# A graph-network kernel whose GpSimd gathers also wait, group by group, for TensorE to be done with the fourth group back

## The chip, the cores and the metric

The kernel runs on one core of one Trainium2 chip. The metric is the device time of one execution in microseconds (us), lower is better. Of the kernel before there are three timed runs and one profiled execution.

## What is computed

Two layers on 6250 nodes of 256 features, in float32. Only the first one matters here:

```python
h = batch_norm(layernorm(x) @ w1.T + b1, g1, bt1)     # 6250 x 256
diff = h[src] - h[dst]                                # 200000 edges, sorted by dst
m = segment_max(diff, dst)                            # per node, 0 where there is no edge
hg = gelu(batch_norm(concat([h, m]) @ wg.T + bg))
x = x + batch_norm(hg @ w2.T + b2) + layernorm(x)
x = x + ffn(layernorm(x))                             # 8 experts, three layers each, softmax weights
```

The costly part is `segment_max` with its 200000 gathered rows of 256 floats.

## The kernel before

**Stages.** The program computes z = layernorm(x) @ w1.T with signs folded in, keeps z in SBUF as high and low float32r parts (`zhl`) and writes it to DRAM (`runs[0:N]`). Then comes the scan that is described below, then the small repair of runs that cross a partition border, the gather of every node's maximum (`gm`), the layer with `wg` and `w2`, and the expert network.

**The scan.** The sorted edges are cut into 128 windows of 1564 consecutive edges, one for each partition. Step s handles edge s of every window: a 128 x 256 tile of z rows, which is combined with the row of the step before by `max(previous + penalty, row)`. The steps go through a ring of 46 slots (`STEPS`) in SBUF, in 34 rounds. A round has seven groups of slots (`NG`, `GS`): 8, 8, 6, 6, 6, 6, 6. In what follows round i and group g have the flat number n = 7i + g.

**Who brings the rows.** GpSimd issues one indirect DMA for each step (L698, `ring<-runs,src_i`), except for the last four slots of group 6 in rounds 1 to 32. Those four come from TensorE (`picked`, L1162 and L1164): for each of the 49 node tiles it multiplies z by a 0/1 matrix of 128 x 512 that says which node each of the 512 wanted rows is. So rounds 1 to 32 have 42 gathers each, and rounds 0 and 33 have 46. The picks run in rounds 0 to 31 (`PK` = 32), always for the round that follows.

**The 0/1 matrices** (`oh`). A group of the scan has seven of them, four made by VectorE (`one_hot`, L921) and three by ScalarE (`distance` L721 and `one_hots` L727). There are buffers for two groups (`HOTS` = 14). TensorE does 28 matmuls of 512 columns for a group: an L1162 and an L1164, twice for each of seven matrices, so 14 of L1164. After the last it adds one to the semaphore `s_ohf`, which is 2 at the start. The makers of group n wait for `s_ohf` at n + 1, that is until group n - 2 is done.

**The order on each engine.**

- GpSimd has only the gathers. Ahead of a group's first gather it waits until the stores of the round before have freed the slots (`s_st[g]`), and ahead of every fourth one until the scan is within 21 steps (`LEAD`, semaphore `s_ch`).
- ScalarE goes group by group (`hots`). Between the parts of the 0/1 matrices it copies ring slots two by two to PSUM (`raw`, L739). The first copy of a group waits for all gathers of that group (`s_g`), and the finished matrices L727 stand behind it in the queue.
- VectorE goes group by group as well (`body`): scan steps (`chain`, L914) take turns with 0/1 matrices, with some counting of edges between them.
- SyncE stores each group of the ring after its last scan step (L845), 1 MB or 768 KB, and streams expert weights in rounds 0 to 15.

```python
if i:
    pool.wait_ge(s_st[g], 16 * i)
for k in range(GO[g], GO[g] + by_pool(i, g)):
    if i and (k - GO[g]) % 4 == 0:
        pool.wait_ge(s_ch, STEPS * i + k - LEAD)
    pool.indirect_dma_start(ring[:, k, :], None, runs[0:N, :], ...).then_inc(s_g[g], 16)
```

The two blocks of functions around the change stand here with their line numbers:

Of the kernel before, what the change touches and what calls it, by code (L numbers as in the profile page):

```python
# [44 lines left out]
NG = 7  # L45
# [8 lines left out]
PK = PG  # L54
SLOTS = 7
BYACT = 4
LEAD = 21
HOTS = 2 * SLOTS
DESCS = 4096
BD = (1, 3, 4, 6)  # L60
# [49 lines left out]
def build(nc, io):  # L110
    ctx = ExitStack()
    with ctx:
# [4 lines left out]
        def sem(name):  # L117

            return spare.pop() if spare else ctx.enter_context(nc.semaphore(name))
# [21 lines left out]
        def sub(base, *names_sizes):  # L141
            at, out = base, {}
            for name, size in names_sizes:
                out[name] = at
                at += -(-size // 64) * 64
                assert at <= plan.top, (name, at, plan.top)
            return out
# [86 lines left out]
        def layer_apply(act, out, arr, c):  # L234

            for t in range(BYACT):
# [8 lines left out]

        places = sub(free0, ("zT", MAT), ("gT", 2 * MAT), ("ring", 0), ("src", WIN * 4), ("pen", WIN * 4), ("oh", HOTS * NPE * P * 4),
                     ("acc", KC * NPE * P * 4), ("part", PW * 4), ("part_hi", PW * 4), ("free", 0))
# [56 lines left out]
        rowf = plan.at("rowf", [1, 2 * P], F32, places["oh"] + 4 * KC * CUT * 4)  # L304
        assert 2 * P <= PIECEW and 4 * KC * CUT * 4 + 2 * P * 4 <= HOTS * NPE * P * 4
        node_i = plan.at("node_i", [P, NT], I32, p2["node"])
# [299 lines left out]

        oh = plan.at("oh", [P, HOTS, NPE * P], F32R, places["oh"])
        ids = plan.at("ids", [P, 2, NPE * P], F32, p2["ids"])
# [31 lines left out]
        s_ohd, s_oha, s_ohf, s_ab, s_pe, s_acc0, s_idp = sem("s_ohd"), sem("s_oha"), sem("s_ohf"), sem("s_ab"), sem("s_pe"), sem("s_acc0"), sem("s_idp")  # L640
# [26 lines left out]
        def by_pool(i, g):  # L667

            return GS[g] - (NPE if g == NG - 1 and 1 <= i <= PK else 0)
# [17 lines left out]
        with nc.Block() as block:  # L687

            @block.gpsimd
            def _(pool):  # L690
                for i in range(ROUNDS):
                    for g in range(NG):
                        if i:
                            pool.wait_ge(s_st[g], 16 * i)
                        for k in range(GO[g], GO[g] + by_pool(i, g)):
                            if i and (k - GO[g]) % 4 == 0:
                                pool.wait_ge(s_ch, STEPS * i + k - LEAD)
                            pool.indirect_dma_start(ring[:, k, :], None, runs[0:N, :],  # L698
                                                    bass.IndirectOffsetOnAxis(ap=src_i[:, STEPS * i + k:STEPS * i + k + 1], axis=0)
                                                    ).then_inc(s_g[g], 16)  # L700

            @block.scalar
            def _(act):
# [104 lines left out]
                def columns(n, k):  # L808
                    act.wait_ge(s_tt, 4 * NCH + KC * n + k + 1)
                    _, _, w = piece_of(n)  # L810
                    for a in range(2):
                        r = act.activation(zs[n % 3][:, a, k, 0:w], ps[:, turned(n, k) + a, 0:w], ACT.Copy)
                    r.then_inc(s_tev, 1)
# [293 lines left out]
            def _(pe):  # L1107
# [68 lines left out]
                pe.transpose(ps[:, 6, 0:P], srcf[:], ident[:]).then_inc(s_srcT, 1)  # L1176
                pe.sem_inc(s_ohf, HOTS // SLOTS)
                for c in range(NCH):
# [914 lines left out]
```

## Time and profile before

| | |
|---|---|
| median of three runs | 3012.4 us (3011.11 to 3012.64) |
| the profiled execution: its own time | 3013.89 us |
| its span, first to last instruction | 3012.1 us |
| mean granted TensorE clock | 0.969 |
| TensorE matmuls busy | 2796.6 us (93%) |
| VectorE busy | 2292.7 us (76%) |
| ScalarE busy | 1943.0 us (65%) |
| GpSimd busy | 1484.6 us (49%) |
| the gathers' first and last start | 89.4 and 1912.5 us |

The profiled execution took 1.8 us more than its span, and 1.5 us more than the median. The profile names engines PE (TensorE matmul), PEld (TensorE weight load), DVE (VectorE), ACT (ScalarE), POOL (GpSimd) and SP (SyncE). A row of instructions says for how long the engine had been idle ahead of it and who ended that. Matmuls overlap in the pipeline, so TensorE's busy time says little of how near it is to its peak. A gather's duration on GpSimd is the time in which the engine made it, and its landing comes later.

### The profile page before, as it was taken

What the parts mean: (1) busy time and instruction counts of PE and PEld (TensorE: products, weight loads), DVE (VectorE), ACT (ScalarE), POOL (GpSimd) and SP (SyncE); (2) the same over time, 40 slices, a digit from 0 to 9 for tenths busy, and PEclk for the clock granted to TensorE, in tenths of its full rate; (3) what the DMA queues carried; (4) which work ended last, traced back from release to release, by engine and by line L of the source; (5) the groups of instructions that cost most, each with busy time, mean ns of one, the idle gap of its engine ahead of it and who ended that gap; (6) DMA issues with size and microseconds to landing.
All of it is one profiled execution on the core that took longest, in us unless ns stands there. A gap on an engine that the chain in (4) does not pass through costs nothing. (4 is left out here: it accounts for less than half of the span.)

```text
span 3012.1 us, 40449 instructions
## 1 busy us (share of the span) xinstructions
PE 2796.6 (93%) x14193; PEld 2342.5 (78%) x14193; DVE 2292.7 (76%) x4785; ACT 1943.0 (65%) x2661; POOL 1484.6 (49%) x1550
## 2 busy tenths in 40 slices
PE   6699999999999999999999998789899999999998
PEld 6577777777776777777777777678799999999998
DVE  6887888888787888887878774498677677676766
ACT  5577777777777777777777765416465565655554
POOL 3677777777777777777777777631000000000000
PEclk9899999999999999999999999899899999999999
DMA  8577777777776666676666666411324334243231
GB/s 252 176 265 231 252 244 244 247 238 247 247 246 233 227 221 224 231 229 223 226 222 222 227 207 214 161 53 75 105 105 142 121 111 136 106 142 117 105 116 56
DMA packets 165632, 560.92 MB, mean 186 GB/s; under 512 B 31278, under 2 KB 68950, under 8 KB 149428
## 3 DMA queue, kind: packets, MB, share of 16 engines
q1 hardware_dynamic: 88164, 356.25, 32.9%
q0 software_dynamic: 77264, 202.08, 23.2%
q8 instruction: 112, 1.84, 0.2%
q14 instruction: 92, 0.75, 0.1%
HBM read 321.21 MB, written 237.00 MB: 185 GB/s over the span
## 5 line engine op out<-in xcount | busy, mean ns | idle before, releaser
L698 POOL DMA_INDIRECT ring<-runs,src_i x1436 | 1386.9, 966 | 469.1 <-issue 365.6
L1162 PE MATMUL ps<-oh,zhl 128*128 128x512 f32 x3136 | 1288.8, 411 | 115.7 <-ACT oh L727 103.4
L1164 PE MATMUL ps<-oh,zhl 128*128 128x512 f32 x3136 | 1245.4, 397 | 0.0
L914 DVE SCALAR_TENSOR_TENSOR ring<-ring,pen,ps 128x256 f32<-128x256 f32 x1260 | 598.8, 475 | 303.9 <-ACT ps L739 286.9
L1162 PEld LDWEIGHTS ps<-oh,zhl 128*128 128x128 f32 x3136 | 602.5, 192 | 284.8 <-ACT oh L727 130.6
L1164 PEld LDWEIGHTS ps<-oh,zhl 128*128 128x128 f32 x3136 | 602.8, 192 | 118.8
L921 DVE TENSOR_SCALAR oh<-ps,nodef 128x512 fp32r<-128x512 f32 x896 | 667.6, 745 | 0.0
L739 ACT ACTIVATE ps<-ring 128x512 f32<-128x512 f32 x630 | 370.4, 588 | 310.7 <-DMA ring<-runs,src_i 287.2
L721 ACT ACTIVATE oh<-ids,nodeneg 128x512 fp32r<-128x512 f32 x672 | 455.9, 711 | 27.0 <-PE ps L1164 26.9
L1707 ACT ACTIVATE av<-ps,vecs 128x896 f32<-128x896 f32 x224 | 246.4, 1100 | 325.3 <-PE ps L204 325.3
L727 ACT ACTIVATE oh<-oh,ones 128x1024 fp32r<-128x1024 f32 x448 | 414.7, 926 | 1.9
L1846 DVE TENSOR_TENSOR h2l<-av,h2h 128x896 fp32r<-128x896 f32 x112 | 122.2, 1092 | 148.4 <-ACT h2h L1709 148.1
L2024 PE MATMUL ps<-fw,h2h 128*128 128x256 f32 x784 | 224.5, 286 | 3.4 <-DVE h2l L1846 3.3
L2025 PE MATMUL ps<-fw,h2l 128*128 128x256 f32 x784 | 222.2, 283 | 0.0
L2026 PE MATMUL ps<-fw,h2h 128*128 128x256 f32 x784 | 222.0, 283 | 0.0
L1648 POOL DMA_DIRECT2D y<-in_x x5 | 8.4, 1685 | 412.1 <-DMA y<-res_d 412.1
L1854 DVE SCALAR_TENSOR_TENSOR y<-ps,wv,y 128x256 f32<-128x256 f32 x392 | 168.7, 478 | 52.6 <-PE ps L2026 52.5
L914 DVE SCALAR_TENSOR_TENSOR ring<-ring,pen 128x256 f32<-128x256 f32 x304 | 146.3, 481 | 76.0 <-DMA ring<-runs,src_i 70.9
L1841 DVE SCALAR_TENSOR_TENSOR y<-bo,wv,y 128x256 f32<-128x256 f32 x392 | 173.6, 479 | 1.4 <-issue 0.2
L202 PE MATMUL ps<-h1h,fw 128*128 128x512 f32 x448 | 168.0, 375 | 2.7 <-DVE h1l L1846 2.7
L203 PE MATMUL ps<-hnl,fw 128*128 128x512 f32 x448 | 164.7, 368 | 0.0
L204 PE MATMUL ps<-hnh,fw 128*128 128x512 f32 x448 | 164.6, 367 | 0.0
(294 smaller groups left out, 3976.1 us busy)
## 6 DMA issues: line engine op xcount, KB each, us to landing
runs<-ring SPq DMA_DIRECT2D x170, 768.0 KB, 3.9
fw<-wsp SPq DMA_DIRECT2D x56, 1536.0 KB, 6.5
runs<-ring SPq DMA_DIRECT2D x68, 1024.0 KB, 4.6
ring<-runs,src_i POOLq DMA_INDIRECT x1436, 3.7
ids<-srcT_d SPq DMA_DIRECT2D x32, 256.0 KB, 5.5
res_d<-x_all SPq DMA_DIRECT2D x7, 896.0 KB
y<-res_d SPq DMA_DIRECT2D x7, 896.0 KB, 8.1
part<-in_Wx SPq DMA_DIRECT2D x16, 384.0 KB, 7.1
```

Source lines behind the costliest of these rows:

```text
L698: pool.indirect_dma_start(ring[:, k, :], None, runs[0:N, :], bass.IndirectOffsetOnAxis(ap=src_i[:, STEPS * i + k:STEPS * i + k + 1], axis= ...
L721: return act.activation(oh[:, hot(i, g, v), :], ids[:, bass.ds(h, 1), :].rearrange("p a n -> p (a n)"), ACT.Abs, bias=nodeneg[:, bass.ds(S ...
L727: act.activation(oh[:, slots, :], oh[:, slots, :].bitcast(F32), ACT.Relu, bias=ones[:, 0:1], scale=-1.0).then_inc(s_oha, 1)
L739: act.activation(ps[:, RAWB[J % 2], :], ring[:, k:k + 2, :].rearrange("p s n -> p (s n)"), ACT.Copy).then_inc(s_cp, 1)
L914: dve.scalar_tensor_tensor(out=ring[:, k, :], in0=ring[:, before, :], scalar=pen[:, STEPS * i + k:STEPS * i + k + 1], in1=row, op0=ALU.add ...
L921: dve.tensor_scalar(oh[:, hot(i, g, v), :], ps[:, IDB, :], nodef[:, SLOTS * g + v:SLOTS * g + v + 1], None, ALU.is_equal).then_inc(s_ohd, 1)
L1162: pe.matmul(ps[:, two + k, :], z_hi(g)[:, v, cols], oh[:, hot(i, g, v), :], start=g == 0 and v == 0, stop=False, skip_group_check=True)
L1164: r = pe.matmul(ps[:, two + k, :], z_lo(g)[:, v, cols], oh[:, hot(i, g, v), :], start=False, stop=False, skip_group_check=True)
L1707: act.activation(av[:, m, :], block_banks(m), ACT.Relu, bias=dv(bi, 2 * e + m), scale=dv(sc, 2 * e + m)).then_inc(s_ev, 1)
L2024: pe.matmul(o, h2h[:, k, st], fw[:, b, 0, 2, k, :], start=k == 0, stop=False)
L2025: pe.matmul(o, h2l[:, k, st], fw[:, b, 0, 2, k, :], start=False, stop=False)
L2026: r = pe.matmul(o, h2h[:, k, st], fw[:, b, 1, 2, k, :], start=False, stop=k == KC - 1)
```

## The change

Ahead of the first gather of every group of rounds 2 to 31, GpSimd also waits for TensorE's semaphore `s_ohf`. The value is 7i + g + 3 - 3 = n. With the 2 it starts from, that asks for n - 2 groups done: groups 0 to n - 3. Counted with group n itself as the first, that is the fourth group back.

```diff
--- before.py
+++ after.py
@@ -55,6 +55,7 @@
 SLOTS = 7
 BYACT = 4
 LEAD = 21
+BEHIND = 3
 HOTS = 2 * SLOTS
 DESCS = 4096
 BD = (1, 3, 4, 6)
@@ -692,6 +693,8 @@
                     for g in range(NG):
                         if i:
                             pool.wait_ge(s_st[g], 16 * i)
+                        if 2 <= i < PK:
+                            pool.wait_ge(s_ohf, NG * i + g + HOTS // SLOTS + 1 - BEHIND)
                         for k in range(GO[g], GO[g] + by_pool(i, g)):
                             if i and (k - GO[g]) % 4 == 0:
                                 pool.wait_ge(s_ch, STEPS * i + k - LEAD)
```

No instruction changes its place on any engine, apart from line numbers. On GpSimd's queue, from the last group of round 1 to the first gather of group 1 of round 2, these rows stand in the kernel before (a gather, its shape, and the semaphores it waits for; `x3` stands for three alike in a row):

```order
L698 DMA ring<-runs,src_i 128x256 [waits s_ch,s_st6]
L698 DMA ring<-runs,src_i 128x256
L698 DMA ring<-runs,src_i 128x256 [waits s_ch,s_st0]
L698 DMA ring<-runs,src_i 128x256 x3
L698 DMA ring<-runs,src_i 128x256 [waits s_ch]
L698 DMA ring<-runs,src_i 128x256 x3
L698 DMA ring<-runs,src_i 128x256 [waits s_ch,s_st1]
```

and these in the changed kernel:

```order
L701 DMA ring<-runs,src_i 128x256 [waits s_ch,s_st6]
L701 DMA ring<-runs,src_i 128x256
L701 DMA ring<-runs,src_i 128x256 [waits s_ch,s_ohf,s_st0]
L701 DMA ring<-runs,src_i 128x256 x3
L701 DMA ring<-runs,src_i 128x256 [waits s_ch]
L701 DMA ring<-runs,src_i 128x256 x3
L701 DMA ring<-runs,src_i 128x256 [waits s_ch,s_ohf,s_st1]
```

Only the first gather of each group has got the new wait beside its two old ones, 210 times in all (30 rounds of seven groups).

## Rows read from the trace of the kernel before

**Rows 1.** The profile's page: busy time of each engine over the span.

```profile
PE 2796.6 (93%) x14193; PEld 2342.5 (78%) x14193; DVE 2292.7 (76%) x4785; ACT 1943.0 (65%) x2661; POOL 1484.6 (49%) x1550
```

**Rows 2.** Groups by line: busy us, mean ns, idle before, who ended it.

```profile
L698 POOL DMA_INDIRECT ring<-runs,src_i x1436 | 1386.9, 966 | 469.1 <-issue 365.6 <-DVE ring L914 71.6 <-POOLq L368 31.9
L1162 PE MATMUL ps<-oh,zhl 128*128 128x512 f32 x3136 | 1288.8, 411 | 115.7 <-ACT oh L727 103.4 <-DVE zhl L969 7.2 <-DVE oh L921 4.3
...
L739 ACT ACTIVATE ps<-ring 128x512 f32<-128x512 f32 x630 | 370.4, 588 | 310.7 <-DMA ring<-runs,src_i 287.2 <-DVE ring L914 23.1
```

**Rows 3.** Waits of GpSimd from 250 to 1800 us: total, times, longest.

```profile
POOL ring L698 <- issue: 309.8, 1017, 0.3
POOL ring L698 <- DVE ring L914: 62.8, 206, 0.3
```

**Rows 4.** Line L698: durations in ns (least, median, most), first and last start.

```profile
L698 POOL DMA_INDIRECT ring<-runs,src_i x1436: 952/957/1670, 89.4 to 1912.5; - x180
...
DMA to landing us min/median/max: 2.7/3.7/6.9
```

**Rows 5.** Windows, line L1164: matmuls begun before a round's first gather starts.

```profile
0.00:202.33 202.33, 65.38 (x164) 31.97 (x164) 0.95 0.69 223
...
0.00:522.02 522.02, 301.70 (x756) 146.54 (x756) 0.96 0.71 236
0.00:575.45 575.45, 338.28 (x846) 164.45 (x846) 0.96 0.72 237
...
0.00:894.79 894.79, 572.64 (x1438) 277.63 (x1438) 0.97 0.72 240
...
0.00:1320.12 1320.12, 883.27 (x2226) 427.57 (x2226) 0.97 0.71 236
...
0.00:1745.38 1745.38, 1194.62 (x3010) 578.10 (x3010) 0.97 0.71 233
```

**Rows 6.** Windows, line L698: gathers begun by the same moment.

```profile
0.00:575.45 575.45, 369.69 (x382) 0.96 0.72 237
```

**Rows 7.** Timeline at the start of round 23, 1319.0 to 1320.3 us.

```profile
1319.48 0.40 PE L1164 MATMUL ps<-oh,zhl 128*128 128x512 f32 x1
...
1319.94 0.39 PE L1164 MATMUL ps<-oh,zhl 128*128 128x512 f32 x1
...
1320.12 0.96 POOL L698 DMA_INDIRECT ring<-runs,src_i  x1 [0.30 <-issue]
```

**Rows 8.** Timeline at 1984 to 1986 us: a gather of `gm` waits for TensorE.

```profile
1984.07 1.69 PE L1408 MATMUL ps<-ident,gm 128*128 128x128 f32 x14
...
1986.03 0.95 POOL L1322 DMA_INDIRECT gm<-runs,pos_i  x1 [1.07 <-PE ps L1408]
```

**Rows 9.** Timeline at 547 to 549 us, group 1 of round 8.

```profile
547.17 0.60 ACT L739 ACTIVATE ps<-ring 128x512 f32<-128x512 f32 x1 [6.72 <-DMA ring<-runs,src_i]
...
548.89 0.79 PE L1162 MATMUL ps<-oh,zhl 128*128 128x512 f32 x1 [5.49 <-ACT oh L727]
```

**Rows 10.** Windows: PE, PEld, DVE, ACT, POOL busy (count), granted clock, DMA share, GB/s.

```profile
330.00:333.00 3.00, 0.55 (x4) 0.12 (x2) 1.14 (x3) 1.77 (x3) 2.39 (x3) 1.00 0.99 385
333.00:336.00 3.00, 3.00 (x8) 2.33 (x8) 3.00 (x9) 2.64 (x5) 2.09 (x3) 0.51 0.56 173
550.00:555.00 5.00, 5.00 (x13) 3.86 (x12) 4.85 (x12) 4.64 (x8) 3.83 (x4) 0.50 0.36 105
703.00:706.00 3.00, 0.58 (x4) 0.15 (x2) 1.19 (x3) 1.82 (x3) 2.34 (x3) 1.00 0.93 380
706.00:709.00 3.00, 3.00 (x14) 2.46 (x15) 3.00 (x9) 2.64 (x5) 2.13 (x3) 1.00 0.57 174
```

**Rows 11.** Timeline at the end of the scan, 1912 to 1919 us.

```profile
1912.47 0.96 POOL L698 DMA_INDIRECT ring<-runs,src_i  x1 [0.30 <-issue]
1916.67 2.57 DVE L914 SCALAR_TENSOR_TENSOR ring<-ring,pen 128x256 f32<-128x256 f32 x5 [4.29 <-DMA ring<-runs,src_i]
...
1918.33 0.69 PE L1232 MATMUL ps<-rowf,ones 1*128 1x256 f32 x2
```

## The prediction

> **What bounds the kernel now.** I read the page first. TensorE is busy for 93% of the span and GpSimd for only 49% [rows 1], which points to TensorE. But GpSimd's work ends at 1912 us [rows 4], and its share is an average over the scan and over stages in which it does next to nothing. So I went on to the groups by line. The 1436 gathers of L698 are busy for 1386.9 us, 966 ns each, and the idle time ahead of them is nearly all "issue", which is time in which the engine waited for nothing the profile shows [rows 2]. The waits of GpSimd from 250 to 1800 us say it more sharply: 1223 gathers, none with more than 0.3 us of idle time ahead of it [rows 3]. None of the old waits holds GpSimd up, neither the one for the stores nor the one for the scan. It makes gathers back to back: (1912.5 - 89.4) / 1435 = 1.270 us each [rows 4]. A round of 42 takes 53.3 us.
>
> The others follow it. ScalarE's copies of ring slots wait 287 us for the gathers to land, and the matrices behind them in the queue make TensorE wait 103 us [rows 2]. In one of these places the copy waits 6.72 us and TensorE then 5.49 us [rows 9]. **So the pace of the scan is GpSimd's, and TensorE has time to spare in it.** Time that GpSimd loses is not won back, because it never runs slower than it can. The stage's end hangs on the same queue: last gather at 1912.5 us, last scan step done at 1916.67 + 2.57 = 1919.2 us, with TensorE done at 1919.0 us [rows 11].
>
> **The change, part by part.** It adds 210 waits and takes nothing away. What counts is whether TensorE has finished group n - 3 when GpSimd comes to group n.
>
> *The waits as instructions.* A group's first gather already had two waits and still shows the 0.30 us of any other [rows 7]. They are worked off while the gather before is busy for 0.96 us. I cost a third one at nothing. Without that cover the nearest price is a whole further gap of 0.3 us, 63 us for 210, but the two old waits together show none of it; below nothing is ruled out, since nothing is taken away.
>
> *Where the wait binds.* For the first group of round i, groups 0 to 7i - 3 must be done: 14 x (7i - 2) matmuls of L1164. A window that ends where the round's first gather starts counts those begun. For round 9 the gathers begun are 46 + 8 x 42 = 382, so the next one is its first [rows 6]. Needed are 854, begun are 846: eight short [rows 5]. The same windows for rounds 2 to 31 (first and last in [rows 5]) give as shortage 4, 0, 0, 0, 1, 4, 0, 8, 0, 0, 0, 7, 0, 4, 0, 6, 1, 1, 2, 4, 0, 0, 1, 7, 0, 1, 7, 0, 0, 0: together 58, in 15 rounds.
>
> Even with none short the last one is mostly still running. At round 23 all 2226 have begun [rows 5], but the last ends at 1319.94 + 0.39 = 1320.33 us and the gather started at 1320.12 [rows 7]: 0.21 us late. This is no accident. Group 6 has only two gathers, so from the last gather of group 4 to the next round's first one there are just nine steps of 1.27 us, about as long as landing, copy, matrix and the 28 matmuls take. In rounds 3 and 11 it is done in time.
>
> At the six other groups of a round, read in the same way, GpSimd comes after TensorE's end, except behind a large disturbance (group 4 of round 8 for one). What is waited for there is then missing at the next round's start, so I count round starts only.
>
> *What a wait costs beyond that.* A gather of `gm` that waited for TensorE started at 1986.03 us, after an end at 1984.07 + 1.69 = 1985.76 [rows 8]: 0.27 us.
>
> *The sum.* Pairs of matmuls follow each other by 1319.94 - 1319.48 = 0.46 us [rows 7].
> - 58 pairs short x 0.46 = 26.7 us
> - 28 rounds x (0.21 + 0.27) = 13.4 us
> - in 15 rounds half a pair more, since the next had not begun: 15 x 0.23 = 3.5 us
>
> That makes 43.6 us. It adds up, because a held gather delays its own group's landing, then ScalarE, then TensorE: TensorE is no earlier at the next round's start, relative to GpSimd, than it was.
>
> *TensorE's clock.* In each round TensorE runs dry ahead of group 1, because group 6 came from two gathers and group 1 needs eight. In round 4 it is busy for 0.55 of 3 us and then at a granted clock of 0.51, so half of 2.4 GHz; in round 11 it is busy for 0.58 of 3 us and stays at 1.00 [rows 10]. Nine rounds (3, 7, 9, 13, 15, 17, 21, 25, 28) are spared the gap today, as TensorE is behind in them. When GpSimd waits for TensorE, they have it too. What such a fall leaves at the next round's start lies between nothing and what followed the fall of round 14: at round 15, 1442 needed and 1438 begun [rows 5], four pairs or 1.8 us. Most falls leave a pair or none, so I take 0.5 us, an estimate: 9 x 0.5 = 4.5 us. If the gap never costs anything it is 0, at 1.8 us each it is 16.
>
> The Trainium skill has a rule that weighs more against this change ("TensorE: Matmul & The Clock Gate", section "HAM oscillation — how this bites in real kernels"): idle gaps between bursts put the array back to half clock every time, and its example spends a quarter of its time so. Gaps of one length went both ways here, so the trace agrees in part. By the rule the time would be that of the first rival below.
>
> In all 43.6 + 4.5 = 48 us. Against the profiled execution's 3013.9 us that is 3062 us; against the median of 3012.4 us it is **3060 us**. Late next is only TensorE's own group 4, and behind the waiting gather stand only gathers. What waits for these is ScalarE, VectorE and the stores, all shifted alike. After round 31 nothing waits any more, and the end of the stage shifts as a whole.
>
> **The rivals.**
>
> *A loop through the clock, 3082 us.* GpSimd's wait makes TensorE's gap, the gap halves its clock, and the late TensorE makes GpSimd wait longer. Today the lateness is worked off, since TensorE's round is shorter than 53.3 us. For it: five pauses like that of round 8, with the clock at 0.50 behind it [rows 10], all leave large shortages. Against it: after most falls one pair or none is short. Price: six rounds at (6.5 x 0.46 + 0.71 =) 3.7 us, and 24 at 2.0 us, between the 0.5 of none short and the 2.5 of four: 70 us.
>
> *Waits that are mostly met, 3040 us.* TensorE's ends are modelled and could lie earlier, and the release of a waiting gather might cost nothing. Then only whole missing pairs count, 27 us.
>
> *It does not bind, 3012 us.* If the value asked for one group less, TensorE would have 14 x 0.46 = 6.4 us more, over the 8 x 0.46 + 0.7 = 4.4 us of the worst round start, and nothing would change. Against it stands the code: `s_ohf` starts at 2.
>
> *Fewer gathers under way help, 2999 us.* No row here names what made the gathers of round 8 land late [rows 9]; it may be the crowd of gathers and stores on the DMA engines. With gathers held back it would thin out, and if what makes some gathers longer than 957 ns (up to 1670 ns [rows 4]) is the crowd too, GpSimd's own pace rises. At most that gives 1436 x (966 - 957) ns = 13 us, and it decides only if the waits cost less than 13 us; the 27 us of whole pairs alone are twice that. The Trainium skill says that the engines alternate between the queues fed by software and by hardware ("DMA: Bandwidth & Descriptors", section "SWDGE vs HWDGE vs iDMA"), which would make holding one back a help to the other. No row tells whether it does so here.
>
> **How the numbers follow.** My own forecast gets 0.66 (its own range is 3050 to 3070 us), the loop 0.22, waits mostly met 0.07, no binding 0.03, and the help 0.02. The range goes from 3039 us, whole pairs alone, to 3084 us, the loop at its price and a little over. It leaves out the last two cases and the worst of the loop. A measurement of this kernel can tell 0.2%, 6 us, from no change. Slower gets 0.95, within 0.2% 0.03, faster 0.02.
>
> **What would show it.** In the profile of the changed kernel GpSimd's gathers should have a new releaser, L1164 of TensorE, about 30 to 40 times, for 40 to 60 us with the 0.3 us of the gap in it, nearly always at a round's first group, by 0.5 us or by 2 to 4 us. The gathers should last 966 ns as before, the last one should start at about 1960 us, and what comes after it should take as long as now. The clock should fall to half in more of the thirty rounds. The prediction is wrong if GpSimd shows no such waits, if they add up to 40 us or more and the scan still ends before 1940 us, or if waits of 2 us and more stand at most round starts.

## The result and the profile after

The changed kernel takes 3080.06 us (median of 4 runs, 3071.94 to 3083.20) against 3012.45 us for the kernel before (4 runs, the three known before and one beside the change, 3011.11 to 3012.64). The ratio is 1.0216, with an interval of [1.0204, 1.0228], so it is slower by 67.6 us. The forecast was 3060 us with a range of 3039 to 3084 us. The side and the bound came out as predicted. The price was 20 us too low, outside the 3050 to 3070 us that the forecast gave its own mechanism.

The page of the changed kernel, busy time of each engine, answers to [rows 1]:

```profile
span 3080.7 us, 40449 instructions
...
PE 2813.0 (91%) x14193; PEld 2362.7 (77%) x14193; DVE 2291.3 (74%) x4785; ACT 1943.7 (63%) x2661; POOL 1484.5 (48%) x1550
```

No engine has more work than before, apart from 16 us more of TensorE (2813.0 against 2796.6 us), yet the span has grown by 68.6 us. The 16 us go with more time at the lower clock, see below. The time is in what stands between the instructions. The groups by line (busy us, mean ns of one, idle time ahead of them and who ended it) answer to [rows 2]. The line numbers have moved by three:

```profile
L701 POOL DMA_INDIRECT ring<-runs,src_i x1436 | 1386.4, 965 | 538.5 <-issue 451.8 <-DVE ring L917 53.3 <-POOLq L369 33.4
L1165 PE MATMUL ps<-oh,zhl 128*128 128x512 f32 x3136 | 1298.4, 414 | 168.4 <-ACT oh L730 156.4 <-DVE zhl L972 6.5 <-DVE oh L924 5.1
...
L742 ACT ACTIVATE ps<-ring 128x512 f32<-128x512 f32 x630 | 370.1, 588 | 377.0 <-DMA ring<-runs,src_i 346.9
```

The gathers themselves have kept their length, 965 ns against 966. The idle time ahead of them has grown from 469.1 to 538.5 us, by 69.4 us. That is the whole loss. ScalarE's copies wait 60 us longer for gathers to land (346.9 against 287.2 us), and TensorE waits 53 us longer for ScalarE's matrices (156.4 against 103.4 us). These are followers of a slower GpSimd, and cost nothing by themselves.

GpSimd's waits over the whole span (total, times, longest) show where the 69.4 us are. [rows 3] showed no idle time above 0.3 us in the scan:

```profile
POOL ring L701 <- issue: 451.8, 1260, 4.5
POOL ring L701 <- DVE ring L917: 53.3, 175, 0.3
POOL ring L701 <- POOLq L369: 33.4, 1, 33.4
```

The row "issue" now has a longest one of 4.5 us. The prediction expected TensorE to be named as the releaser. The profile does not name it: it puts the new waits under "issue", time in which nothing visible was waited for. They are found only by the length of the gap. Thirty-seven gathers of the changed kernel stand behind a gap of more than 0.4 us. Less the 0.3 us that every gather has, these holds add up to 68.0 us: 59.0 us at group 0 (29 holds), 5.4 us at group 4 (6 holds), 3.6 us at group 1 (2 holds). All of them are at a group's first gather, where the new wait stands.

Line L701 alone (least, median and longest duration in ns, first and last start; then from issue to landing) answers to [rows 4]:

```profile
L701 POOL DMA_INDIRECT ring<-runs,src_i x1436: 951/957/2606, 90.8 to 1981.3; - x180
...
DMA to landing us min/median/max: 2.7/3.2/7.4
```

The last gather starts at 1981.3 us instead of 1912.5, 68.8 us later, and the span has grown by 68.6 us. What follows the scan takes as long as it did. Holds, last gather and span all say 68 to 69 us.

**One hold closely.** The first group of round 13 is n = 91, so TensorE's groups 0 to 88 have to be done. A window that ends while that gather is held shows all of them begun: 14 x (7 x 13 - 2) = 1246 matmuls of L1167.

```profile
0.00:816.30 816.30, 497.96 (x1246) 242.45 (x1246) 0.95 0.70 232
```

The timeline has the last of them and the gather that waits for it (start, duration, then in brackets the idle time ahead):

```profile
816.16 0.39 PE L1167 MATMUL ps<-oh,zhl 128*128 128x512 f32 x1
...
817.29 0.96 POOL L701 DMA_INDIRECT ring<-runs,src_i  x1 [3.43 <-issue]
```

The matmul ends at 816.16 + 0.39 = 816.55 us and the gather starts at 817.29. So a released gather comes 0.74 us after TensorE's end in the records. The prediction had 0.27 us, from [rows 8]. In the 29 holds at group 0 it is 0.74 us, in the eight at groups 1 and 4 it is 0.99 and 1.03 us: 29 x 0.74 + 8.2 = 29.7 us in all. The remaining 38.3 us are lateness of TensorE: 37.6 us at group 0, and less than 1 us at the other two together. At group 4 five of the six held gathers would have started after TensorE's recorded end, and were held all the same.

ScalarE shows that the end in the records is not what is late. At the end of an earlier group its next 0/1 matrix waits for the same semaphore:

```profile
524.98 0.39 PE L1167 MATMUL ps<-oh,zhl 128*128 128x512 f32 x1
...
525.41 0.72 ACT L724 ACTIVATE oh<-ids,nodeneg 128x512 fp32r<-128x512 f32 x1 [0.90 <-PE ps L1167]
```

It starts at 525.41 us, 0.04 us after 524.98 + 0.39 = 525.37, and so it does in all 15 such places.

**Where the release is spent.** The trace also holds what GpSimd's sequencer does, the part of the engine that takes the instructions in ahead of it. The waits for `s_ch`, and now those for `s_ohf` too, do not stand on the gather: they stand in an instruction of the sequencer's own, `EVENT_SEMAPHORE`, ahead of it. The gather itself carries the wait for `s_st[g]`. Durations of these instructions in ns (least, median, longest), in the kernel before and in the changed one:

```profile
L697 POOLq EVENT_SEMAPHORE  x231: 17/17/17, 141.7 to 1890.5; - x116
```

```profile
L700 POOLq EVENT_SEMAPHORE  x231: 17/3867/13445, 142.9 to 1959.0; - x116
```

Their number is the same, and so is that of all instructions (40449): the new wait has gone into an instruction that was there already. In each of the 37 holds it ends 0.04 us after TensorE's matmul, as fast as ScalarE. The gather starts 0.70 us after that at group 0, and 0.94 to 0.99 us after it at groups 1 and 4. So the release is not late in reaching GpSimd. It is spent between the sequencer's wait and the gather. In the kernel before this wait is over 10.6 us or more ahead of its gather, and nothing of it is seen. In the changed one the first gather of round 3, with 0.72 us between them, is not held, and those with 0.70 us are. Why the groups differ is not known.

**Where TensorE is late.** Round 14 shows the place the prediction spoke of under the clock. ScalarE's first copy and TensorE's next matmul, with their idle time, and the two stretches of 3 us around them (busy time of PE, PEld, DVE, ACT and POOL, then TensorE's clock, the DMA share and GB/s):

```profile
896.49 0.60 ACT L742 ACTIVATE ps<-ring 128x512 f32<-128x512 f32 x1 [5.92 <-DMA ring<-runs,src_i]
...
898.21 0.79 PE L1165 MATMUL ps<-oh,zhl 128*128 128x512 f32 x1 [5.04 <-ACT oh L730]
```

```profile
894.00:897.00 3.00, 0.00 (x0) 0.00 (x0) 0.00 (x0) 0.51 (x1) 2.39 (x3) 0.98 0.92 320
897.00:900.00 3.00, 1.79 (x4) 1.49 (x5) 2.88 (x6) 3.00 (x6) 2.35 (x3) 0.50 0.42 132
```

The copy waited 5.92 us for gathers to land while the DMA engines were 92% busy, TensorE had nothing to do for 5.04 us, and then it went on at a granted clock of 0.50, which is 1.2 of 2.4 GHz. TensorE has gaps of over 4 us ahead of group 0 or 1 in 15 rounds, before in five. The mean granted clock fell from 0.969 to 0.959. In rounds 2 to 31 the clock records hold 139.9 us at half clock in 27 stretches, against 81.9 us in 17 in the kernel before.

Still, TensorE's lateness itself has hardly grown. Read from the trace of the kernel before in the same way, as the end of the last matmul needed less the start of the round's first gather, it is 34.3 us in 28 rounds; in the changed kernel it is 37.6 us. With 0.74 us for each release the old trace alone would have given 55.5 us at the round starts, where 59.0 were measured.

### The profile page after: what moved, and what is told of

Same layout as the page of the kernel before. It is cut to its first block and busy times, and to the rows that moved or that the text cites. A ratio compares the mean times of both kernels' runs of the same rounds, so it can differ in the third digit from the quotient of the medians.

```text
span 3080.7 us, 40449 instructions
## 1 busy us (share of the span) xinstructions
PE 2813.0 (91%) x14193; PEld 2362.7 (77%) x14193; DVE 2291.3 (74%) x4785; ACT 1943.7 (63%) x2661; POOL 1484.5 (48%) x1550
## 5 line engine op out<-in xcount | busy, mean ns | idle before, releaser
L701 POOL DMA_INDIRECT ring<-runs,src_i x1436 | 1386.4, 965 | 538.5 <-issue 451.8
L1165 PE MATMUL ps<-oh,zhl 128*128 128x512 f32 x3136 | 1298.4, 414 | 168.4 <-ACT oh L730 156.4
L1167 PE MATMUL ps<-oh,zhl 128*128 128x512 f32 x3136 | 1256.2, 401 | 0.0
L1165 PEld LDWEIGHTS ps<-oh,zhl 128*128 128x128 f32 x3136 | 610.1, 195 | 330.3 <-ACT oh L730 109.3
L1167 PEld LDWEIGHTS ps<-oh,zhl 128*128 128x128 f32 x3136 | 610.5, 195 | 122.3
L742 ACT ACTIVATE ps<-ring 128x512 f32<-128x512 f32 x630 | 370.1, 588 | 377.0 <-DMA ring<-runs,src_i 346.9
```

The lines of the kernel that those rows point to most:

```text
L701: pool.indirect_dma_start(ring[:, k, :], None, runs[0:N, :], bass.IndirectOffsetOnAxis(ap=src_i[:, STEPS * i + k:STEPS * i + k + 1], axis= ...
L742: act.activation(ps[:, RAWB[J % 2], :], ring[:, k:k + 2, :].rearrange("p s n -> p (s n)"), ACT.Copy).then_inc(s_cp, 1)
L1165: pe.matmul(ps[:, two + k, :], z_hi(g)[:, v, cols], oh[:, hot(i, g, v), :], start=g == 0 and v == 0, stop=False, skip_group_check=True)
L1167: r = pe.matmul(ps[:, two + k, :], z_lo(g)[:, v, cols], oh[:, hot(i, g, v), :], start=False, stop=False, skip_group_check=True)
```

## The experiments

The question was what the 68 us consist of: whether holds add up one to one, what the release is worth, what makes TensorE late (clock or late landings), and whether the wait as an instruction costs anything. The theory that I held, "the count": GpSimd sets the pace, each hold costs TensorE's lateness plus a release, and nothing comes back. The rivals held that it feeds itself through the clock, or that something else than the holds costs the time. The diffs are against the changed kernel.

**A condition of the chip first.** In two of the four batches the kernel before itself took 3589 and 3586 us instead of 3008 to 3015. The results give the chip the number 0 in one of these two batches and in both of the others, and 4 in the second of the two. Whether the number 0 is always the same chip is not on record, so it stays open whether this goes with the chip or with a state of it. Those runs can't be set against the others, so they stand apart, at the end of this section.

### The wait in every fourth round only

```diff
-                        if 2 <= i < PK:
+                        if 2 <= i < PK and i % 4 == 2:
```

> The new wait is kept in rounds 2, 6, 10, 14, 18, 22, 26 and 30 alone. In the kernel before TensorE was 2.1, 0.8, 0.2, 0.2, 0.5, 0.3, 0.2 and 0.4 us behind GpSimd at the starts of these rounds (4.7 us together). Theory C, a hold breeds the next: a hold moves the gathers behind it into other transfers, TensorE runs dry for longer, its clock falls, and it is late again one round on. With three rounds between two holds this has died out, so each costs its own lateness and 0.73 us: 8 x 0.73 + 4.7 = 10.5 us, 3019 to 3027 us. Rival D, each hold costs the same 2.1 us that the changed kernel shows on average, whatever came before: 17 us, 3029 us.

Measured: 3023.62 us against 3008.00 for the kernel before (7 runs), ratio 1.0051 [1.0034, 1.0068], so 15.6 us. GpSimd's waits over the whole span:

```profile
POOL ring L701 <- issue: 382.0, 1207, 2.4
POOL ring L701 <- DVE ring L917: 69.5, 228, 0.3
POOL ring L701 <- POOLq L369: 32.0, 1, 32.0
```

There are 13 holds with 14.2 us: eight at group 0 (10.1 us, as theory C had it) and five at group 4 (4.1 us), which neither theory had. The 15.6 us lie inside the range of C, but nearer to the 17 us of D than to the 10.5 us of C, so the time alone does not decide between them. Idle time ahead of the gathers is 382.0 + 69.5 + 32.0 = 483.5 us, 14.4 over [rows 2]. In the three rounds between, where TensorE could catch up, nothing of it came back, though TensorE has the time. That is as the count says. Against the trace of the kernel before the span has grown by only 9.1 us, since the gathers of this batch were shorter (953 against 957 ns in the median, 4.9 us in sum). A round with the wait costs 15.6 / 8 = 2.0 us, and 67.6 / 30 = 2.3 us where all have it. So rounds may disturb their neighbours a little, by 0.3 us.

### A tighter wait

```diff
-BEHIND = 3
+BEHIND = 2
```

> The wait asks for one group more, n - 2. TensorE ends a group 6.5 to 7.5 us after the one before, so at a round start a gather is held for another 7 us, and at other groups, where 1.6 to 7 us were to spare, for up to 5 us. By this 30 x 7 = 210 us and more come on top of the changed kernel: 3290 to 3500 us. If holds were hidden by work that GpSimd or the others catch up with, it would stay under 3200 us.

Measured: 3727.93 us (3684.58 to 3731.09), ratio 1.2347 [1.2268, 1.2426], 719.9 us slower. The expectation, 3290 to 3500 us, was far too low. GpSimd's waits over the whole span, and then 70 us of the scan (same columns as above):

```profile
POOL ring L701 <- issue: 1120.9, 1319, 13.2
POOL ring L701 <- DVE ring L917: 35.4, 116, 0.3
POOL ring L701 <- POOLq L369: 33.5, 1, 33.5
```

```profile
1000.00:1070.00 70.00, 49.92 (x189) 37.93 (x188) 40.95 (x88) 37.69 (x57) 35.98 (x38) 0.83 0.49 170
```

133 holds take 719.3 us. All engines are idle for a good part of these 70 us, TensorE for 20 of them, and its clock is at 0.83 of full; over the whole span it is 0.886. GpSimd waits for TensorE and TensorE then for the gathers, and in rounds 2 to 31 the clock is at half for 731 us (82 us in the kernel before). That is what the loop of my first rival would look like; how much of the 720 us is the clock and how much the mutual waiting was not separated. I had counted the waits with the group times of a TensorE that is mostly at full clock. One to one it still is: the idle time ahead of the gathers grew by 1189.7 - 469.1 = 720.6 us.

### The stores made small, without and with the new wait

Each group stores its last slot only, and the whole of `runs` is written once after the scan. The contents of `runs` are then not the real ones, so what is computed from them is left out, and both kernels are longer than theirs by the late writes. They are to be compared with each other. Both have this edit, the second one has the new wait as well:

```diff
-                    sp.dma_start(run_rows(STEPS * i + GO[g], GS[g]),
-                                 ring[:, GO[g]:GO[g + 1], :].rearrange("p s n -> p (s n)")).then_inc(s_st[g], 16)
+                    sp.dma_start(run_rows(STEPS * i + GO[g + 1] - 1, 1),
+                                 ring[:, GO[g + 1] - 1:GO[g + 1], :].rearrange("p s n -> p (s n)")).then_inc(s_st[g], 16)
...
+                for i in range(ROUNDS):
+                    sp.dma_start(run_rows(STEPS * i, STEPS), ring[:].rearrange("p s n -> p (s n)")).then_inc(s_st[0], 16)
+                sp.wait_ge(s_st[0], 32 * ROUNDS)
```

> The kernel before, with each store of a group cut to its last step (128 KB in place of 768 KB or 1 MB), and all of the runs' memory written once after the scan, from whatever the ring holds then. What it leaves out: the right contents of the runs, so the maxima are not computed. It is the reference for the next kernel and says what the stores do to the gathers. Theory C (gathers of groups 0 to 2 land late because of the stores): last gather of group 1 to first copy at 2.8 to 3.1 us in all rounds, with none of the 5.4 to 6.0 us of rounds 8, 12, 16, 20 and 24, and the scan's last gather at 1912 us as before, since GpSimd sets the pace. If the late landings have another cause, they stay.

> The changed kernel with the same cut stores (and the same part left out). Theory C: without the stores' crowd a hold breeds nothing, so each round costs TensorE's constant lateness of 0.2 us and the 0.73 us of the release, perhaps less, since landings are shorter: GpSimd is held for 15 to 35 us in all, and it is slower than the kernel with cut stores and without the wait by as much. Theory K (the clock alone breeds the longer holds, the stores have nothing to do with it): 60 to 70 us, as with full stores.

Measured: 3484.36 us (3480.72 to 3485.96) without and 3521.22 us (3518.08 to 3526.15) with the wait, 36.9 us more; in the profiled executions 42.9 us more. ScalarE's waits for landed gathers in rounds 2 to 31, first in the kernel before, then with small stores and no new wait (total, times, longest):

```profile
ACT ps L739 <- DMA ring<-runs,src_i: 283.4, 133, 6.7
```

```profile
ACT ps L739 <- DMA ring<-runs,src_i: 285.5, 135, 4.0
```

The total is the same but the longest is 4.0 us instead of 6.7. From the last gather of group 1 to its first copy it now takes 2.7 to 3.1 us in every round; the 5.4 to 6.0 us of some rounds are gone. So it was the stores of 768 KB to 1 MB beside them that made those landings late, which [rows 9] had left open. GpSimd's waits over the whole span, without and with the new wait:

```profile
POOL ring L698 <- issue: 361.2, 1185, 0.3
POOL ring L698 <- DVE ring L917: 76.2, 250, 0.3
POOL ring L698 <- POOLq L368: 33.4, 1, 33.4
```

```profile
POOL ring L701 <- issue: 421.5, 1237, 3.2
POOL ring L701 <- DVE ring L920: 60.4, 198, 0.3
POOL ring L701 <- POOLq L369: 32.0, 1, 32.0
```

31 holds take 44.7 us, of which 30 x 0.74 + 0.99 = 23.3 us are release and 21.4 us lateness. That is between the two expectations, 15 to 35 us and 60 to 70 us. Against the 68.0 us with full stores, 23 us of the change's cost come from the large stores: a late landing makes ScalarE's matrices late, then TensorE, then the next round's first gather. Most of this is there without the new wait: TensorE's lateness at the round starts is 34.3 us in the kernel before and 14.6 us with small stores. With the wait it is 37.6 and 22.4 us. What the new wait adds in time at half clock is much the same, from 51.2 to 116.1 us with small stores and from 81.9 to 139.9 us with full ones, so that is not the difference. How far the stores' late landings act through the clock (81.9 against 51.2 us without the new wait) was not separated.

### Zero matmuls in TensorE's idle time

On top of the change, 16 and 32 matmuls of 128 columns with zeros stand ahead of groups 0 and 1. They add nothing to the result and give the array work where it ran dry.

```diff
+                        if 2 <= i and g < 2:
+                            for f in range((16, 32)[g]):
+                                pe.matmul(ps[:, two, 0:P], zr[:], zr[:], start=False, stop=False, skip_group_check=True)
```

> The changed kernel, with 16 and 32 matmuls of 128 zero columns on TensorE ahead of groups 0 and 1 of rounds 2 to 31, where it runs dry. They add zeros to the sums, so nothing of the result changes. Theory: of the 68 us of holds about 17 come from the half clock behind these gaps. If the fillers keep the clock up in the thirty rounds, a hold is shorter by 0.5 us in the mean and the kernel takes 1.014 to 1.020 of before on a chip where that takes 3008 to 3013 us. Rival: the clock does not matter there, and the fillers only add 2 to 4 us a round to TensorE's own work, which makes it later at the next round's start: 1.024 of before and more. On a chip where the kernel before takes about 3587 us, TensorE is what bounds: 0.967 to 1.00 of before, and nothing on the clock follows.

Measured: 3080.87 us (3075.83 to 3096.27, 5 runs) against 3014.57 (3010.22 to 3015.20, 9 runs), ratio 1.0231 [1.0207, 1.0254]. The gathers' group, and rounds 2 to 31 of this kernel in one window:

```profile
L701 POOL DMA_INDIRECT ring<-runs,src_i x1436 | 1386.0, 965 | 546.6 <-issue 456.6 <-DVE ring L917 56.6 <-POOLq L369 33.4
```

```profile
206.00:1880.00 1674.00, 1578.29 (x8044) 1252.21 (x8043) 1290.29 (x2798) 1171.36 (x1774) 1214.40 (x1263) 0.97 0.67 223
```

The time at half clock in these rounds fell from 139.9 to 85.3 us, about what the kernel before has, and the mean granted clock is back at 0.969. TensorE's gaps of over 4 us ahead of group 0 or 1 fell from 15 rounds to four. The holds went up all the same, to 39 with 76.1 us, of which 44.8 us are lateness (38.3 in the changed kernel). If falls of the clock had bred the holds, these should have shrunk. The ratio lies between the two expectations, nearer to the rival's 1.024. The run does not clear the clock altogether: the zero matmuls take some 67 us of TensorE in these rounds (1578.29 us busy here, 1511.14 in the same rounds of the changed kernel), and what they won in clock they may have lost in time. What it does show is that fewer falls alone bring nothing here.

### One to one

Idle time ahead of the gathers, less that of the kernel before, against the time lost, for all runs in the first condition:

| kernel | idle over that of before | time over that of before, medians | of the profiled executions' spans |
|---|---|---|---|
| the change | 538.5 - 469.1 = 69.4 us | 67.6 us | 68.6 us |
| every fourth round | 483.5 - 469.1 = 14.4 us | 15.6 us | 9.1 us |
| `BEHIND = 2` | 1189.7 - 469.1 = 720.6 us | 719.9 us | 712.2 us |
| small stores, with and without | 513.9 - 470.8 = 43.1 us | 36.9 us | 42.9 us |
| zero matmuls | 546.6 - 469.1 = 77.5 us | 66.3 us | 72.6 us |

From 14 to 720 us, what GpSimd is held for is what the end loses, within 2 us in the first three rows, by medians. By spans the second and third are 5 and 8 us lower, because the gathers of their batch were shorter by 4.9 and 8.3 us in sum. The last two rows have medians 6 and 11 us lower; their profiled executions were above their medians by 4.9 and 5.6 us, and by spans they agree within 5 us.

In part this is bookkeeping: the first gather's start, the gathers, the idle time between them and what follows the last one make up the span. What the runs add is that the other terms stay. What follows the last gather's start takes 1099.3 to 1099.6 us in the first three and the kernel before, and 1571.6 and 1572.4 us with small stores; with the zero matmuls it is 1095.3 us, which makes up most of the 5 us in that row. And no other idle time of GpSimd shrinks when a hold comes, because there was none above 0.3 us in the scan.

### The runs in the other condition

Five edits were run there, two of them twice, each against the kernel before in the same batch. The wait at all groups but a round's first:

```diff
-                        if 2 <= i < PK:
+                        if 2 <= i < PK and g:
```

> The new wait is left out at the first group of each round and kept at the other six. In the changed kernel 59.0 of the 68.0 us in which gathers were held stand at first groups. Theory A, the cost arises at round starts, where only nine gathers lie between TensorE's group and the waiting one: few waits bind, 3013 to 3025 us. Rival B, the lateness of TensorE is what costs, and what is not waited for at a first group is waited for at the second or fifth: TensorE's lateness in the kernel before of up to 4.4 us would return there, 3030 us and more.

> No new wait at the first group of each round, all others kept. On a chip where the kernel before takes 3008 to 3013 us, theory A (the cost arises at round starts): 1.000 to 1.004 of before, under 10 us of holds. Rival B (TensorE's lateness is paid elsewhere): 1.006 and more. On the other kind of chip: 0.96 again.

Measured: 3457.09 us against 3588.97, ratio 0.9629 [0.9590, 0.9669], and in the second batch 3447.57 against 3585.82, 0.9622 [0.9575, 0.9668].

The wait at a round's first group alone:

```diff
-                        if 2 <= i < PK:
+                        if 2 <= i < PK and g == 0:
```

> The new wait is kept at the first group of each round alone. Theory A: nearly all of the loss remains, 3070 to 3082 us, with 30 holds. Rival B, the waits at the other groups matter by themselves (as instructions, or by what they shift): 3055 to 3065 us.

Measured: 3901.31 us (3897.23 to 3908.97), ratio 1.0862 [1.0820, 1.0903].

The new wait directly ahead of the gather, behind the one for the scan:

```diff
-                        if 2 <= i < PK:
-                            pool.wait_ge(s_ohf, NG * i + g + HOTS // SLOTS + 1 - BEHIND)
...
                                 pool.wait_ge(s_ch, STEPS * i + k - LEAD)
+                            if 2 <= i < PK and k == GO[g]:
+                                pool.wait_ge(s_ohf, NG * i + g + HOTS // SLOTS + 1 - BEHIND)
```

> The same waits in another order: the new one stands directly ahead of the gather, behind the two old ones. In the changed kernel a held gather starts 0.73 us after TensorE's end, where 0.27 us had been priced. If the missing 0.46 us are spent on the wait that stands between, a held gather starts after about 0.27 us and 30 to 37 holds are shorter by 0.46 us each: 3064 to 3068 us. If the slow part is the release by this semaphore itself, nothing changes: 3072 to 3083 us, still 0.73 us.

> The new wait directly ahead of the gather, behind the two old ones. On a chip where the kernel before takes 3008 to 3013 us: if the missing 0.46 us of a release are spent on the wait that stands between, a held gather starts 0.27 us after TensorE's end and the kernel is 12 to 17 us faster than the changed one: 1.017 to 1.019 of before. If the release itself is slow, 0.73 us and 1.020 to 1.024.

Measured: 3487.52 us, 0.9723 [0.9681, 0.9765], and 3478.66 us, 0.9704 [0.9666, 0.9742]. A held gather starts 0.78 us after TensorE's end in 41 holds of the two runs, against 0.74 us in 20 holds with the old order in the same condition. The edit did not put the new wait onto the gather, though. In the trace the instruction ahead of the gather still carries `s_ohf` and `s_ch`, only in the other order, and the gather still carries `s_st[g]`. The gather starts 0.70 us after that instruction's end, as before. So the order of the two waits within it is worth 0.04 us, and where the 0.46 us go was not tested by this edit.

A wait that is always met, for ten groups back:

```diff
-BEHIND = 3
+BEHIND = 10
```

> The new wait asks for group n - 10 in place of n - 3, which TensorE has long released. Only the 210 waits as instructions are left. Expected by all theories so far: no gather is held and the time is that of the kernel before, 3010 to 3015 us. If a third wait costs issue time, it shows as gaps over 0.30 us and up to 0.1 us for each: up to 3033 us.

Measured: 3592.98 us (10 runs), 1.0006 [0.9986, 1.0025]. Since GpSimd has time to spare in this condition, as will be seen, this alone does not show that the waits cost nothing. Its profile stands below for that of the kernel before in this condition.

And the change itself, unaltered:

> The changed kernel again, beside the kernel before on the same chip. The last four kernels ran on a chip on which the kernel before takes 3589 us in place of 3012 us, and there the waits in groups 1 to 6 (0.963 of before) and all waits with the new one last (0.972) were faster than none. Theory of pace: where GpSimd makes gathers without a pause (kernel before at 3008 to 3013 us), the change costs 2.0 to 2.4%. Where GpSimd is held anyway (kernel before at about 3590 us, 514 us of waits for the scan), its pace is not the bound, and the same change gives 0.96 to 1.00 of before.

Measured: 3466.98 us (3460.90 to 3483.05) against 3585.82, ratio 0.9671 [0.9630, 0.9711]. **The same change that costs 2.2% in the first condition gains 3.3% in this one.** The expectations written before the first batch of this condition did not have that, since they were argued from a GpSimd that sets the pace. The one above, written after it, had 0.96 to 1.00.

GpSimd does not set the pace here. TensorE's row for what it waited for up to 2500 us, in the kernel with the wait that is always met (total, times, longest), then in the change:

```profile
PE ps L1165 <- issue: 167.4, 136, 4.5
PE ps L1167 <- issue: 162.6, 139, 3.1
```

```profile
PE ps L1165 <- issue: 167.2, 77, 6.0
PE ps L1167 <- issue: 53.6, 41, 2.9
```

TensorE stands idle for nothing that the profile shows, for 167.4 + 162.6 = 330.0 us. The timeline of the former shows what such a place looks like, and the window over it the other engines:

```profile
1064.85 0.58 PE L1167 MATMUL ps<-oh,zhl 128*128 128x512 f32 x1 [0.98 <-issue]
1066.95 0.58 PE L1165 MATMUL ps<-oh,zhl 128*128 128x512 f32 x1 [1.51 <-issue]
1069.06 0.59 PE L1167 MATMUL ps<-oh,zhl 128*128 128x512 f32 x1 [1.52 <-issue]
```

```profile
1065.00:1070.00 5.00, 1.85 (x4) 0.82 (x4) 0.08 (x1) 0.00 (x0) 1.40 (x2) 0.50 0.23 70
```

One matmul comes every 2.1 us, where two come in 0.46 us otherwise [rows 7], and everything else stands behind it. There is one such stretch in nearly every round, mostly in group 1 or 2. A group of 28 with one takes 12 to 22 us, once 54 us, instead of 7.0 us in the median. GpSimd then has to wait for the scan, as its own rows say in the kernel whose new wait is always met:

```profile
POOL ring L701 <- DVE ring L917: 514.3, 174, 46.7
POOL ring L701 <- issue: 393.3, 1248, 1.9
POOL ring L701 <- PE ps L1167: 35.6, 13, 9.5
```

It has time to spare here, so holding it costs little. Some 75 us of what this condition costs come after the last gather (1175 us to the end, 1100 otherwise). In the rows above, "issue" also counts single waits ahead of a group's first matmul. The pauses inside a group, which the first condition does not have at all, are set against the spans here:

| kernel, in this condition | pauses inside groups | span |
|---|---|---|
| wait always met | 309 us | 3593.4 us |
| the change | 108 us | 3467.4 us |
| no wait at group 0, two runs | 112 and 113 us | 3453.1 and 3449.4 us |
| new wait last, two runs | 74 and 105 us | 3475.5 and 3473.3 us |
| wait at group 0 alone | 436 us | 3901.2 us |

The kernels with few such pauses are the fast ones, but not one to one: from the first row to the last the pauses grow by 127 us and the span by 308 us. So the waits at groups 1 to 6 go together with fewer of these pauses, and the wait at group 0 alone with more. Why they arise, and why the waits change them, stays open. The gathers last as long as in the first condition (965 ns), and TensorE's matmuls are some 5% longer (431 against 411 ns at L1165), at a mean granted clock of 0.893.

### What was not tried

In the first condition: leaving out the wait at group 0, the wait that is always met, `BEHIND = 4`, and the zero matmuls on the kernel before. In neither condition was there a kernel whose gather carries the new wait itself, as the one of `gm` does. No version beat the kernel before in that condition.

## Why the prediction was right, and where it was off

**The bound.** GpSimd's pace sets the scan's end: right, by the table above. The reading of an engine with a share of 49% as the one that sets the pace is what carried the forecast. ("Nearly all issue" was 365.6 of the 469.1 us in [rows 2]; the rest of the gaps, put down to VectorE, are of the same 0.3 us.) The Trainium skill advises otherwise ("Perfetto Trace Analysis", section "Identifying the Most-Contended Engine"): look for the engine with the highest occupancy, which for GpSimd and VectorE is the busy share. By that VectorE with 76% comes ahead of GpSimd with 49% [rows 1], and a wait on GpSimd looks free. The trace disagrees, and not only over the whole span: from 202.33 to 1800.04 us VectorE is busy for 81% and GpSimd for 76%, and still it is GpSimd's lost time that the end loses.

**The waits as instructions: nothing.** Right. The 173 first gathers that have the new wait and are not held come 0.30 or 0.31 us after the one before, as with two waits. The trace says why: the new wait shares an instruction with the one for `s_ch`, so there is no instruction more.

**Where it binds.** It was said to be round starts only. 29 of 30 round starts have a hold, with 59.0 of the 68.0 us. The other 9.0 us are at group 4 and group 1. The prediction left these out, as missing at the next round's start anyway. In the every-fourth-round run five holds at group 4 cost 4.1 us, and the total still agreed with the end one to one, so they add up. Of the 9.0 us 8.2 are release: these gathers are held although TensorE is hardly late there. With a release of 0.27 us six of these eight holds would be 0.3 us or less.

**The lateness.** The forecast had 26.7 + 28 x 0.21 + 3.5 + 4.5 = 40.6 us, clock included. Measured are 38.3 us. Of the 4.5 us for what the wait itself adds, 37.6 - 34.3 = 3.3 us came. The count of matmuls begun at the time of the first gather was good to a few us, although some 20 us of it hang on the stores and so on landings (34.3 against 14.6 us), which the prediction left without a price of their own.

**The release: this is the term that was mis-sized.** It stood as 28 x 0.27 = 7.6 us and measures 29.7 us, 37 holds at 0.74, 0.99 or 1.03 us. The 22 us between them are the whole error (48.1 + 22.1 - 2.3 = 67.9 us). The 0.27 us came from one gather of `gm` [rows 8]. That it was released by TensorE is not in doubt: it is 0.27 us for the same gather in all fourteen traces that are kept, and the landing that this gather depends on came 7 us earlier (1979.15 us in the kernel before). What differs is where the wait stands. The gather of `gm` carries it itself; in the scan it stands in the sequencer's instruction ahead, and 0.70 us or more pass between the two. That this is the cause is read from the records; no run moved the wait. The prediction took the price from a wait of another form, as a value without a range.

The Trainium skill has a part of the answer ("Perfetto Trace Analysis", section "Summary: the profiler window per engine type"): TensorE's end is an estimate, and the passing on of the semaphore is not in the profile. The trace agrees only in part. ScalarE, released by such a matmul, starts 0.04 us after that end, GpSimd's sequencer goes on 0.04 us after it, and the gather starts 0.74 us after it; 0.70 us of that are GpSimd's own.

**The clock.** The falls came, from 17 to 27 stretches where nine more were forecast, and the mean clock went from 0.969 to 0.959. Their price could not be told from that of late landings, but the two together added 3.3 us of lateness at the round starts. The experiment that took the falls away brought nothing back. The loop through the clock (3082 us) lies nearest to the measured time, and yet it is not what happened. It needed six rounds at 3.7 us and all others at 2.0; its 70 us have no larger release in them, and the measured 68 us have 29.7 us of it. That the result lies inside the range of 3039 to 3084 us is luck to that extent: the upper end came from this rival's price, and the time got there by the release. The Trainium skill's rule on idle gaps ("TensorE: Matmul & The Clock Gate", section "HAM oscillation — how this bites in real kernels"), which the prediction held against its own sum, would have given this rival's time. The trace has the gaps and more of the falls, but a lateness that grew by 3.3 us, and the run with the zero matmuls (0.969 again, and still 66 us slower), speak against the clock as what decides here.

**Fewer gathers under way help.** It did nothing here: 965 ns against 966. In the other condition the change did help, by 119 us, while its gathers were only 6 us shorter in sum than with the wait always met, so not in this way.

**The forecast's signs.** Fulfilled: 37 holds (30 to 40), almost all at a round's first group, gathers of the same length, the same time behind the scan, the clock down in more rounds. Not fulfilled: TensorE as the named releaser, 40 to 60 us in all with the 0.3 us of the gap in it (68.0 + 37 x 0.3 = 79 us), and the last gather at 1960 us (1981.3). One sign of being wrong came true: with the gap in it, as the profile shows it, waits of 2 us and more stand at 17 of 30 round starts. Less the gap there are 13, and one of 1.99 us. That is what a release looks like that is 0.47 us longer than priced.

## What to carry to other kernels

An engine with a share of 49% can set the pace: look for back-to-back instructions with no idle time above their usual gap, and then price every new wait on that engine one to one. Count each wait twice, once for how late the other engine is and once for the release, and take the release from a wait of the same form: see whether the semaphore stands on the waiting instruction itself (0.27 us here) or in one of the sequencer's ahead of it (0.74 to 1.03 us here). If the trace has none of that form, put the two as ends. A wait binds as soon as its release comes too late, so count also the places where the other engine is done just in time. And state the condition: a verdict on a wait holds only as long as the same engine sets the pace.

## What the runs showed of the hardware that was not expected

- A gather on GpSimd that waits for TensorE starts 0.74 us after the matmul's end in the records, in some cases 0.99 or 1.03 us, where the wait stands in an instruction of GpSimd's sequencer ahead of it. It starts after 0.27 us where it carries the wait itself. ScalarE starts after 0.04 us. The profile calls a hold of the first kind "issue".
- In some rounds the last gather of group 1 reaches its first copy after 5.4 to 6.0 us; with stores of 128 KB in place of 768 KB to 1 MB beside the gathers it is 2.7 to 3.1 us in every round.
- There is a condition in which the kernel before takes 3586 to 3589 us instead of 3012, with stretches of matmuls 2.1 us apart and nothing waited for, and in which the change's sign turns: 0.9671 instead of 1.0216.
